# Two token dispatches written as loops over four groups of eight tiles

## The reference, cut to what matters

```python
t = t + ffn(layernorm(t))
# in ffn, for each token:
logits = t @ router                       # 8 experts
weights, experts = top_k(logits, 2)       # two experts per token, with weights
out = sum over the two of  weight * (gelu(t @ W1[e] + b1[e]) @ W2[e] + b2[e])
```

## Time and profile before

| what | us |
|---|---|
| median of three runs | 2409.54 |
| the profiled execution's own time | 2423.15 |
| its span, first to last instruction | 2421.1 |
| layer 0's dispatch, in the span | 1350.4 to 1478.5 |
| layer 1's dispatch, in the span | 1854.8 to 1985.0 |
| mean granted clock of TensorE | 0.907 |

### The profile page before, as it was taken

One profiled execution on the slowest core, in us unless ns is written; L12 is line 12 of the kernel. 1 busy time (PEld: TensorE's weight loads), 2 busy tenths in 40 slices (PEclk: granted clock), 3 DMA queues, 4 the chain that ended last, 5 costly groups with the idle time before them and its releaser, 6 DMA issues. The chain is left out here.

```text
span 2421.1 us, 84549 instructions
## 1 busy us (share of the span) xinstructions
PE 2004.5 (83%) x29091; PEld 1533.1 (63%) x29092; DVE 2012.4 (83%) x3575; ACT 1767.4 (73%) x2810; POOL 843.7 (35%) x598
## 2 busy tenths in 40 slices
PE   4749999999999999999996525975897229999995
PEld 3427666666666666666664414862585219999995
DVE  5869999999999999999997654759798638888883
ACT  5669999999999999999995643646687516666662
POOL 6324324213233422311332254540264733333331
PEclk9969999999999999999998657985898559999997
DMA  2013232322323232232322333433113712222225
GB/s 83 1 35 92 73 92 71 88 77 75 90 73 92 71 90 75 77 89 73 92 73 81 122 109 107 141 115 131 38 69 134 221 60 48 49 48 48 48 49 155
DMA packets 296697, 203.14 MB, mean 84 GB/s; under 512 B 153579, under 2 KB 277958, under 8 KB 296358
## 3 DMA queue, kind: packets, MB, share of 16 engines
q1 hardware_dynamic: 276838, 166.33, 24.5%
q0 software_dynamic: 19776, 35.73, 5.6%
HBM read 64.79 MB, written 112.92 MB: 73 GB/s over the span
## 5 line engine op out<-in xcount | busy, mean ns | idle before, releaser
L597 DVE TENSOR_TENSOR plow<-prob 128x1024 f16<-128x1024 f32 (+1 forms) x1024 | 1127.8, 1177 | 4.4 <-ACT prob L520 4.2
L520 ACT ACTIVATE prob<-scores 128x1024 f32<-128x1024 f32 x1024 | 999.7, 1025 | 89.7 <-PE scores L640 58.7
L660 PEld LDWEIGHTS outp<-vs,prob 128*128 128x128 bf16 x7680 | 515.5, 98 | 280.1 <-issue 220.5
L660 PE MATMUL outp<-vs,prob 128*128 (+1 forms) x7680 | 604.1, 193 | 24.7 <-DVE plow L597 12.0
L640 PE MATMUL scores<-qT,kT 128*128 (+1 forms) x2048 | 611.3, 380 | 7.5 <-DMA kT<-shift_rows 2.8
L662 PE MATMUL outp<-vs,plow 128*128 (+1 forms) x7680 | 601.5, 193 | 0.0
L473 POOL TENSOR_TENSOR osum<-osb 128x128 f32<-128x128 f32 x64 | 289.2, 4519 | 776.1 <-DVE rec L602 776.1
L662 PEld LDWEIGHTS outp<-vs,plow 128*128 128x128 f16 x7680 | 503.0, 97 | 58.3 <-issue 0.3
L1566 POOL DMA_INDIRECT token_sums<-m1eyo,m1edest x71 | 134.6, 1896 | 277.5 <-DVE m1eyo L1531 156.2
L1401 PE MATMUL m1eph<-m1exT,m1ew1c 128*128 128x128 f16 x3408 | 204.3, 220 | 0.0
L1401 PEld LDWEIGHTS m1eph<-m1exT,m1ew1c 128*128 128x128 f16 x3408 | 195.4, 99 | 0.5
(11 more groups left out here) (395 smaller groups left out, 3408.6 us busy)
## 6 DMA issues: line engine op xcount, KB each, us to landing
sorted_rows<-zero SPq DMA_DIRECT2D x128, 522.0 KB, 4.6
staged<-qk SPq DMA_DIRECT2D x73, 128.0 KB, 2.4
m0exr<-sorted_rows SPq DMA_DIRECT2D x71, 130.5 KB
m1exr<-sorted_rows SPq DMA_DIRECT2D x71, 130.5 KB, 2.4
ls_got<-expert_rows SPq DMA_DIRECT2D x8, 1024.0 KB, 5.6
na_staged<-in_L_ffn_W_dram SPq DMA_DIRECT2D x16, 512.0 KB, 3.1
m1dstg<-in_L_ffn_W_dram SPq DMA_DIRECT2D x16, 512.0 KB
tok<-in_x_dram SPq DMA_DIRECT2D x8, 512.0 KB, 9.1
```

The source lines that it names most:

```text
L520: act.activation(prob[g % PBUF][:, :], scores[g % 2][:, :], ACT.Exp, scale=1.0 / (QK_SCALE * QK_SCALE)).then_inc(prob_ready, 1)
L597: dve.tensor_tensor(l[:, 0:n], p[:, 0:n], high(p)[:, 0:n], ALU.subtract).then_inc(low_ready, 1)
L660: pe.matmul(to, high(prob[g % PBUF])[:, cols], v, start=(g == 0 and i == 0 and j == 0), stop=False, skip_group_check=True)
```

## The change

Both dispatches become loops of four rounds (`Fori`) on TensorE, ScalarE and VectorE; GpSimd and SyncE stay written out. In a round:

- VectorE does eight `prepare`, then `route(g)`, then four `low`.
- ScalarE does `normed` and `take` of the eight tiles with the table switch behind the fifth tile's `take`, then `weigh` (layer 1), four `high`, and in layer 0 eight `add_normed`.
- TensorE does eight `turn` and `mult`, then `rank(g)`.

So no tile of group g + 1 is prepared before `route(g)`. Waits and addresses that depend on the tile are now computed from the loop's register. The logits have one PSUM buffer and not two. `mask` covers one group; the counts `seen` are summed up by two instructions behind the slots, and `rank` waits for them. There are four staging buffers. The rows of the ring come free by a count: behind tile t (t = 3 to 18) GpSimd waits until tile t - 3 has landed and raises `freed` by one (BEHIND = 3); `prepare(t)` waits for `freed` of at least t + 1, with 16 given at the start. Work on the first bias goes behind the loop. The diff, cut to its core:

```diff
+    NB = 4
+    BEHIND = 3
-        pl = [ps(f"pl{u}", A) for u in range(2)]
+        pl = ps("pl", A)
...
-            def prepare(t):
-                row = halves[:, t % RING, :]
+            def prepare(t, u, half):
+                row = halves[:, ds(half * G + u, 1), :].squeeze(1)
                 dve.wait_ge(xn_ready, t + 1)
-                if t >= RING:
-                    dve.wait_ge(sent[t % RING], 16 * TOP * (t // RING))
+                dve.wait_ge(freed, t + 1)
...
+                dve.tensor_copy(slots[:, ds(half, 1), :, :].squeeze(1), place[:, :, :]).then_inc(slots_ready, 1)
+                link(dve.tensor_reduce(more[:, :], mask[:, :, :].rearrange("p t e -> p e t"), AX.X, ALU.add))
+                link(dve.tensor_tensor(seen[:, :], seen[:, :], more[:, :], ALU.add))
+                dve.sem_inc(counted, 1)
...
-            for t in range(NT):
-                prepare(t)
...
-                if t in route_after:
-                    route(route_after[t])
-                for i in parts_after(t - LAG):
-                    low(i)
+            with dve.Fori(0, NGR) as g:
+                for u in range(G):
+                    prepare(g * G + u, u, g % 2)
+                route(g, g % 2)
+                dve.sem_clear(step)
+                for j in range(NB):
+                    low(g * NB + j, j)
...
+            with act.Fori(0, NGR) as g:
+                act.wait_ge(scaled, g + 1)
+                for u in range(2):
+                    normed(g * G + u, u)
+                for u in range(G):
+                    if u + 2 < G:
+                        normed(g * G + (u + 2), u + 2)
+                    take(g * G + u, u)
+                    if u == NX:
+                        act.activation(warm[:, :], eps[:, :], ACT.Exp)
+                if sums_dram is not None:
+                    weigh(g, ds(g * G, G))
+                for j in range(NB):
+                    high(g * NB + j, j)
+                if add_norm:
+                    for u in range(G):
+                        add_normed(g * G + u)
...
+            with pe.Fori(0, NGR) as g:
+                turn(g * G, 0, g % 2)
+                for u in range(G):
+                    if u + 1 < G:
+                        turn(g * G + (u + 1), u + 1, g % 2)
+                    mult(g * G + u, u)
+                rank(g)
...
+                if BEHIND <= t < NT - RING + BEHIND:
+                    pool.wait_ge(sent[(t - BEHIND) % RING], 16 * TOP)
+                    pool.sem_inc(freed, 1)
```

More of the change, by code:

```diff
@@ L893, in dispatch @@
         place = sb("place", [P, TOP, G])
-        slots = [sb(f"slots{u}", [P, TOP, G], I32) for u in range(2)]
-        seen = [sb(f"seen{u}", [P, E_N], F16) for u in range(2)]
+        slots = sb("slots", [P, 2, TOP, G], I32)
+        seen = sb("seen", [P, E_N], F16)
+        more = sb("more", [P, E_N])
         cnt = sb("cnt", [P, E_N])
-        over = sb("over", [P, E_N, S // ET])
         stops = [sb(f"stops{u}", [P, E_N]) for u in range(2)]
         tiles = sb("tiles", [P, E_N])
-        past = sb("past", [P, MAXT, E_N])
         owner = sb("owner", [P, MAXT])
@@ L942, in dispatch, with part @@
         block = ctx.enter_context(nc.Block())
[L944 to L961, removed]
+        NP = NB * NGR
+        assert NP == TOP * E_N
+        def part(i, j):
+            e, half = i // TOP, j % TOP
+            if narrow and half == 0:
+                src, split, n0, n1 = w1_dram, (w1[:, ds(e, 1), 0], w1[:, ds(e, 1), 1]), 0, KB
+            else:
+                n1 = NF if narrow else (half + 1) * NF // TOP
+                n0 = 0 if narrow else half * NF // TOP
+                src, split = w2_dram, (w2[:, 0, ds(e, 1)], w2[:, 1, ds(e, 1)])
+            buffer = stg[j].rearrange("p (a b) -> p a b", a=n1 - n0)
+            rows_of = src[ds(e, 1)].squeeze(0).rearrange("(k p) f -> p k f", p=P)[:, n0:n1, :]
+            return rows_of, buffer, *(x.squeeze(1)[:, n0:n1, :] for x in split)
         @block.sync
@@ L972, in _ @@
             sp.dma_start(b1n[:, :], b1_dram if narrow else b1_dram.rearrange("e (n p) -> (e n) p", p=P)).then_inc(b_in, 16)
[L973 to L983, removed]
+            for i in range(NP):
+                if i >= NB:
+                    sp.wait_ge(w_split, i - NB + 1)
+                rows_of, buffer, _, _ = part(i, i % NB)
+                sp.dma_start(buffer, rows_of).then_inc(w_in[i % NB], 16)
+                if sums_dram is not None and i == NB - 1:
                     store = lambda t0, t1: sp.dma_start(
@@ L1040, in choose @@
                 link(dve.tensor_reduce(code[:, i, :], tmp[:, :, :], AX.X, ALU.max))
[L1041 to L1047, removed]
+                link(dve.tensor_tensor(hot[:, i, :, :], per_expert(first), per_tile(code[:, i, :]), ALU.is_equal))
@@ L1048, in route @@
+            def route(g, half):
+                group = ds(g * G, G)
+                top = [best[:, i, group] for i in range(TOP)]
+                tail = tails[:, ds(half * G, G), :]
+                dve.wait_ge(multiplied, g * G + G + 2)
+                logits = pl[:, :, :]
                 if gate_bias_dram is not None:
@@ L1199, in _ @@
                 act.activation(sd[:, c], mv[:, c, 1], ACT.Sqrt, bias=eps[:, 0:1]).then_inc(rooted, 1)
-            act.wait_ge(scaled, 1)
-            normed(0)
-            normed(1)
-            for t in range(NT):
-                if t + 2 < NT:
-                    if t + 2 == G:
-                        act.wait_ge(scaled, 2)
-                    normed(t + 2)
-                take(t)
-                if t == G - 1 and narrow:
-                    act.wait_ge(b_in, 16)
-                    act.activation(b1h[:, :], b1n[:, :], ACT.Copy, scale=W_SCALE).then_inc(b_high, 1)
-                if t == 2:
-                    act.activation(warm[:, :], eps[:, :], ACT.Exp)
-                if add_norm and t >= G:
-                    add_normed(t - G)
-                for i in parts_after(t):
-                    high(i)
-                if t + 1 in route_after and t + 1 < NT - 1 and sums_dram is not None:
-                    weigh(route_after[t + 1])
+            act.sem_inc(xt_ready, 2)
```

173 lines of the change are left out of this document (85 added, 88 removed).

## The result

The changed kernel took 2469.8 us (four runs, 2467.37 to 2471.34), the kernel before 2409.65 us beside it (2407.86 to 2413.06): a ratio of 1.0232, interval 1.0209 to 1.0256, slower by 60 us. The direction was right, the size was not: 2418.5 us was forecast, with 2431 as the upper end. The profiled execution took 2469.12 us (span 2467.4), 46.0 us more than that of before. The other 14 us come from the kernel before, which varies: beside the later experiments its medians were 2414.1 to 2421.0 us and single runs 2406.6 to 2428.5, so the 2423.15 us of its profile lie inside what it does without a change.

A forecast was written before the change was run, and what follows sets the result against it. Each dispatch was start-up, 64 DMAs and GpSimd's pauses for slots (25.1 us in both). Terms -2.9 + 2.8 + 5.7 + 2 = +7.6, with 1.4 us for a late tile +9, gave 2418.5 us; 8-in-10 range 2386 to 2431.

The forecast's parts named there:

- What bounds it, and lateness: Both dispatches: start-up, 64 DMAs and pauses, together 25.1 us; TensorE's news up to 12 us late under back-to-back GpSimd DMAs.
- The period under lateness: GpSimd's group plus 1.5 us plus route: 26.9 us in layer 0, 28.4 in layer 1; three periods +2.8 and +5.7 us.
- rival B: Dispatch periods: lateness takes each of the last tiles; six periods 3 us above forecast, 2437 us; chance 0.08.
- Smaller terms of the period: In a dispatch period: route and hand-over 4.3 us (layer 0) and 6.0 (layer 1); GpSimd's group in layer 1 20.9 us.
- Computed addresses: In the loops: 57 ns each, run ahead of the instruction before; nothing, at most 8.6 us for six periods if exposed.
- Start-up: Both dispatches: route(0) follows tile 7, not 10, gaining 1.5 and 0.8 us, plus 0.3 us each for counts; -2.9 us.
- Table load in each round: ScalarE in each round: one table switch of 1.28 us, if executed there, counted in the period.
- undisturbed sum: A group's period without lateness: 18.0 us in layer 0; 21.4, with ScalarE's extra 22.8 us, in layer 1.
- Added waits of GpSimd: GpSimd's 16 waits and 16 increments per dispatch: 2 us for both, 0.06 us per pair; at most ten.
- the back edges (C): Loops on three engines: forecast nothing; the rival has 18 back edges at up to 1 us, +15, 2433 us; chance 0.04.
- The 13.6 us between profile and median: Whole kernel: the median stands 13.6 us under the profiled execution, carried over unchanged to give 2418.5 us.

The follow-up runs named there:

- a1: The changed kernel with its three loops written out four times, same order and waits, constant addresses: 2454.1 us, ratio 1.0144 to the kernel before.
- d1: The changed kernel with ScalarE's one table switch ahead of the loop, not inside it: 2467.3 us, ratio 1.0231 to the kernel before.
- a4: The changed kernel with each round's four weight parts between the tiles, not behind the route; still loops: 2467.0 us, ratio 1.0210 to the kernel before.
- c3: a4 with one more VectorE instruction (128x1024, unused data) behind each low part in layer 0: 2461.3 us, ratio 1.0181 to the kernel before.
- b3: The changed kernel with eight more matmuls into an unused bank behind each tile's transposes: 2486.0 us, ratio 1.0268 to the kernel before.
- a3: The changed kernel with GpSimd waiting once per group until tile 4's two DMAs have landed: 2458.3 us, ratio 1.0162 to the kernel before.
- c1: The kernel before with a tile's logits from four matmuls of 16 columns, not eight of 8: 2409.3 us, ratio 0.9977 to the kernel before.

## Why the prediction was wrong

- **What bounds it, and lateness.** Right. Breaks, spread parts and long instructions of VectorE all act on the same pauses, and the clock (0.50 in these stretches) and the DMAs' pace stayed as they were.
- **The period under lateness. This step failed.** It read "the last tile's news therefore comes when GpSimd stops, plus 1.5 us", and put 26.9 and 28.4 us. Measured: 31.9 us (95.7 / 3) and 34.4 us (103.3 / 3). A tile's transposes start only behind the copy of the tile two before, and its own copy came up to 10 us after them; so tiles pass one in 5.7 us while GpSimd issues, and three to four of them were left when it stopped (50 matmuls against 18). The term "plus 1.5 us" measured 4.8 to 6.2 us in layer 0 and 6.0 in layer 1, some 26 us too little over the six periods. That the new group would be at its fifth or sixth tile when lateness begins was right. What followed is rival B's mechanism, a backlog that outlasts GpSimd. I priced it at 3 us a period (+27 in all) and gave it 0.08; the periods measured +41.6 us in the profiles, with the loops' part in it, and the whole kernel +60 by the medians.
- **Smaller terms of the period.** Route and hand-over were put at 4.3 and 6.0 us and took 5.1 and 6.4. GpSimd's group in layer 1 was put at 20.9 us, though the 48 DMAs of the earlier trace rows had taken 69.2, or 23.1 a group; it took 22.0.
- **Computed addresses, priced at nothing, 8.6 us at most.** Also wrong: the loops cost 15.7 us by a1's median and 21 by its ratio. From VectorE's cast to its subtraction it is 0.44 us in the loop (1377.00 to 1377.44) and was 0.33 written out (1373.91 to 1374.24 in the trace of before), where I had the computing hidden behind the cast. That this is the cost of the loops is not shown.
- **Start-up, -2.9 us.** Measured +0.4 and +1.4 us. Written out (a1) it is -1.1 and -0.3; a table load ahead of the first tile (1.28 us a dispatch, gone in d1) and the loops took the rest back.
- **Table load in each round**, 1.3 us in the undisturbed sum: it happens and is hidden (d1).
- **Added waits of GpSimd, +2 us; the back edges (C), nothing.** The gaps between DMAs stayed at 0.30 us, so the waits cost nothing that shows. C's price of 15 us was met by the loops as a whole, its mechanism was not seen: VectorE does not idle behind its branch.
- **The 13.6 us between profile and median**, carried over unchanged: they were no constant. Before's own spread covers them, and the changed kernel's profiled execution (2469.12) lies at its median.

What stays open: why TensorE's instructions and news come so late under GpSimd's DMAs, what sets the 0.7 us, and whether it is their issuing or their landing that counts. What speaks for issuing is that a VectorE instruction which only stretches one DMA lets TensorE through (a4's layer 1, c3).

## What to carry to other kernels

Where news arrives late, count how often a chain still has to wait for it, tile by tile and with its number of buffers, and multiply; don't add the lateness once. The instruction counts in a pause (50 matmuls against 18) say how much work was left, and before the change they could have been compared with what the new order leaves. Work done ahead of a serial choice is cover: two tiles of it were worth 0.8% here, and a loop that starts each round from nothing gives it away.

## What the hardware showed that I had not expected

- Under GpSimd's indirect DMAs, one in 1.28 us, TensorE's matmuls started 0.7 us apart (b3), and its semaphore updates came up to 15 us after the modelled end (a4). In a gap of 2.3 us between two DMAs one came after 1.4 us, and the next tiles went at their usual pace of 1 us (a3).
- A VectorE instruction of 1.22 us (128x1024, two inputs) stretches a GpSimd DMA from 0.97 to 2.0 us, and TensorE gets through beside it; with ones of 0.69 us (128x512) the DMAs beside them stayed at 0.97 us in a4's layer 0.
- Four matmuls of 16 columns in place of eight of 8 took 0.23% off the kernel before (c1, interval 0.07 to 0.39%); its profile has shorter pauses.
